# One core, two transformer layers in fp32: the first batch's query tiles go between its key steps, and the second batch's input is normalised late

## The chip, the cores and the metric

The program runs on one core of a Trainium2 chip. A core has TensorE (PE, matrix products, with the queue PEld for its weight loads), VectorE (DVE), ScalarE (ACT), GpSimd (POOL) and SyncE (SP, which here only issues DMAs). Each engine works through its own list of instructions in order, and semaphores tie the lists together. PE writes to PSUM, eight banks of 512 fp32 columns; POOL reads and writes SBUF only. The metric is the device time of one execution in microseconds. The kernel before took 934.42 us, the median of 3 runs (934.37 to 938.33).

## The reference

Two layers work on x, 2 batches of 1024 rows of 128. What the change touches is the attention of the first layer, on the input's layer norm:

```python
xn = _layernorm(x, ln_scale, ln_bias)
q = (xn @ Wq).reshape(b, n, HEADS, d).transpose(0, 2, 1, 3)      # 16 heads of 64
k, v = jnp.split(xn @ Wkv, 2, axis=-1)                            # 4 groups of 64 each
q = _layernorm(q, qn_scale, qn_bias)                              # per head
k = _layernorm(k, kn_scale, kn_bias)
dots = jnp.einsum('bghqd,bgkd->bghqk', qg, k) * d ** -0.5         # 4 heads share a group's keys
attn = jax.nn.softmax(dots, axis=-1)
out = jnp.einsum('bghqk,bgkd->bghqd', attn, v)                    # then out @ Wout, added to x
```

Behind it come a mixture of 8 experts (2 chosen per batch), a gated attention unit in chunks of 64 rows and a gated feed-forward layer with integer weights. They are the same in both kernels.

## The kernel before

Each batch goes through three stages, and the second batch's follow the first's.

**Head.** The rows are normalised over 128 columns (`normalise`, after a power -0.5 on POOL in `root`) and turned by PE (`turn_x`). Keys and values are made in four steps of 256 rows (s = 0 to 3): PE projects (`keys_values`, into two PSUM banks, `kv_at`), ACT squares the keys and keeps the values, DVE sums the squares of each head (`sum_keys`), ACT guesses the inverse root by a logarithm and an exponential (`guess_keys`), DVE mends the guess in three small instructions (`newton`) and multiplies (`normal_keys`, which writes every head twice, side by side: 1008 columns), PE turns the result (`turn_keys`), ACT keeps it rounded (`high_keys`, kh) and DVE the rest (`low_keys`, kl). Queries are made in eight tiles of 128 rows (j = 0 to 7): PE projects the centred weights (`norms`, whose squares give the rate) and the weights folded with the scales (`folded`); ACT squares, DVE sums, ACT guesses, and the product with the rate is made by DVE straight from PSUM for j = 0 to 3 (`normal_queries`) and by POOL for j = 4 to 7, from a copy that ACT makes (`keep_folded`, `rate`). Then PE turns (`turn_queries`), ACT keeps qh, DVE ql. In the first batch DVE also makes the biases (`shifts`), POOL folds the weights (`fold`), PE turns the later layers' weights (`turn_w`), and the second batch's input is normalised by POOL, turned and kept.

**Row maxima.** For j = 4 to 7 PE makes between the projections two score blocks each (`unit_scores`: 128 queries of two heads by 512 keys); DVE takes each block's largest (`largest`), two blocks give a row's maximum, and SP places it by DMA in ql, so that the exponent is taken of scores less their maximum.

**Attention.** 16 slots (`SLOTS`), each two query tiles of one group, in four phases, 64 and the overhang in all. A phase has on PE two score blocks, two key tiles of scores for an earlier slot (`tile_scores`, three products of high and low parts) and two of value products (`tile_values`); ACT takes the exponentials (`exps`), POOL adds them up in five adds of 1024 columns and one of a tail that DVE adds (`add_tail`). Four phases later PE adds up over the rows (`add_up`), ACT inverts (`invert`), DVE corrects and scales (`correct`, `scale`), PE projects (`project_out`), DVE adds to x (`add`). The order on each engine is written out by hand in its `produce` and `attention`; a phase number is `ph`, and slot m's key tiles start at ph = 4m + 5 (`LAG`).

## Time and profile before

| | |
|---|---|
| Median of 3 runs | 934.42 us |
| Profiled execution: time, span | 934.55 us, 932.8 us |
| Mean granted clock | 0.963 of full |
| PE busy | 849.1 us, 91% |
| DVE busy | 638.1 us, 68% |
| POOL busy | 548.5 us, 59% |
| ACT busy | 457.7 us, 49% |

The shares are means over stages that differ. The first batch's head and maxima lie from 5 to 98 us, its attention to 384, the second batch's head and maxima to 461, its attention to 755, and the later layers behind. The time outside the span is 1.75 us. A clock of 0.5 in a stretch is TensorE's lower level, 1.2 GHz, and 1.0 the upper, 2.4 GHz.

### The profile page before, as it was taken

Reading aid. Unit: us, or ns where it says so; the run is one execution under the profiler, and the core shown is the slowest. Engines: PE = TensorE matmul, PEld = TensorE weight load, DVE = VectorE, ACT = ScalarE, POOL = GpSimd, SP = SyncE. Lnnn points to the kernel's source line nnn. Section 1 sums busy time; section 2 is a strip of 40 time slices with the busy share of each in tenths; the row PEclk is TensorE's granted clock in tenths of the full one; section 3 lists DMA queues with packets and bytes.
Section 4 is the critical chain, followed back from the end, with each engine's and each line's share of the span. In section 5 each row is a group of like instructions: output and inputs, shape, how many; then the busy total and the mean of one; then the engine's idle time right before and its main releaser. Section 6 shows DMA issues by size and latency. Waiting matters only on the chain. (4 is left out here: it accounts for less than half of the span.)

```text
span 932.8 us, 13290 instructions
## 1 busy us (share of the span) xinstructions
PE 849.1 (91%) x4792; PEld 442.0 (47%) x4792; DVE 638.1 (68%) x1060; ACT 457.7 (49%) x822; POOL 548.5 (59%) x319
## 2 busy tenths in 40 slices
PE   2797999999999999989799999999999937998598
PEld 2554444444444444544444444444444413784355
DVE  6887667777777775488677777777776354255853
ACT  2465455555555556555455555555555514435232
POOL 3323688688868878403476887788778821247400
PEclk9899999999999999999899999999999966999799
DMA  5000000000000000000000000000000002000001
GB/s 161 1 0 1 1 1 1 1 2 1 1 1 1 1 1 2 1 1 1 1 1 1 2 1 1 2 1 1 1 1 1 1 26 68 1 2 0 0 1 46
DMA packets 49595, 7.96 MB, mean 9 GB/s; under 512 B 42486, under 2 KB 47994, under 8 KB 49530
## 3 DMA queue, kind: packets, MB, share of 16 engines
q1 hardware_dynamic: 48666, 6.99, 4.7%
q8 instruction: 38, 0.62, 0.3%
q14 instruction: 27, 0.22, 0.1%
q10 hardware_dynamic: 864, 0.13, 0.1%
HBM read 5.92 MB, written 1.05 MB: 7 GB/s over the span
## 5 line engine op out<-in xcount | busy, mean ns | idle before, releaser
L977 DVE TENSOR_REDUCE part<-psum 128x2 f32<-128x1024 f32 x256 | 313.3, 1224 | 137.5 <-PE psum L511 137.5
L399 POOL TENSOR_TENSOR space<-space 128x1024 f32<-128x1024 f32 x160 | 380.6, 2379 | 38.3 <-ACT space L752 20.5
L752 ACT ACTIVATE space<-psum 128x512 f32<-128x512 f32 x512 | 264.5, 602 | 156.4 <-PE psum L531 155.5
L546 PE MATMUL psum<-space,vb 128*64 128x512 f32 x1024 | 247.7, 605 | 0.0
L511 PE MATMUL psum<-kh,qh 64*128 64x512 f32 x512 | 128.5, 498 | 13.8 <-DVE part L977 13.4
L404 POOL TENSOR_TENSOR space<-space 128x1024 f32<-128x1024 f32 x30 | 71.6, 2385 | 106.2 <-DVE space L991 106.2
L511 PEld LDWEIGHTS psum<-kh,qh 64*128 64x128 f32 x512 | 48.2, 185 | 154.4 <-DVE part L977 120.3
L546 PEld LDWEIGHTS psum<-space,vb 128*64 128x64 f32 x1024 | 62.4, 136 | 106.5 <-issue 101.1
L531 PE MATMUL psum<-qh,kh 64*128 64x512 f32 x512 | 103.5, 401 | 0.0
L531 PE MATMUL psum<-ql,kh 64*128 64x512 f32 x512 | 102.4, 396 | 0.0
L531 PE MATMUL psum<-qh,kl 64*128 64x512 f32 x512 | 101.9, 394 | 0.0
L420 PE MATMUL psum<-wproj,xnt 128*128 128x512 f32 (+1 forms) x192 | 78.0, 544 | 0.9 <-DVE space L959 0.7
L1297 POOL TENSOR_TENSOR inv<-inv,half_power 128x4 f32<-128x4 f32 (+1 forms) x16 | 19.2, 1203 | 88.0 <-DVE inv L1581 76.4
L531 PEld LDWEIGHTS psum<-qh,kh 64*128 64x128 f32 x512 | 49.2, 189 | 12.9 <-issue 3.6
L531 PEld LDWEIGHTS psum<-qh,kl 64*128 64x128 f32 x512 | 49.1, 188 | 11.7
L531 PEld LDWEIGHTS psum<-ql,kh 64*128 64x128 f32 x512 | 48.9, 188 | 11.1
L420 PEld LDWEIGHTS psum<-wproj,xnt 128*128 128x128 f32 x192 | 35.9, 200 | 24.4 <-issue 20.4
L759 ACT ACTIVATE space<-psum 128x512 f32<-128x512 f32 x32 | 19.2, 601 | 56.2 <-PE psum L574 54.3
L991 DVE TENSOR_TENSOR space<-space 128x512 f32<-128x512 f32 x60 | 44.6, 746 | 2.9 <-ACT space L752 2.9
L766 ACT ACTIVATE space<-psum 128x512 f32<-128x512 f32 x32 | 19.2, 599 | 55.4 <-PE psum L561 55.4
L574 PEld LDWEIGHTS psum<-wout,space 128*64 128x64 f32 x512 | 30.0, 137 | 22.7 <-issue 17.1
L574 PE MATMUL psum<-wout,space 128*64 128x128 f32 x512 | 33.6, 273 | 4.5 <-DVE space L1006 4.5
(164 smaller groups left out, 887.6 us busy)
## 6 DMA issues: line engine op xcount, KB each, us to landing
ql<-nmx SPq DMA_DIRECT2D x256, 0.5 KB, 2.0
w1s<-in_L_ffn_W SPq DMA_DIRECT2D x4, 256.0 KB, 2.7
w2s<-in_L_ffn_W SPq DMA_DIRECT2D x4, 256.0 KB
out<-x SPq DMA_DIRECT2D x4, 256.0 KB, 2.1
x<-in_L_attn_x SPq DMA_DIRECT2D x2, 256.0 KB, 4.4
wproj<-in_L_attn_Wq SPq DMA_DIRECT2D x1, 512.0 KB, 6.7
x<-in_L_attn_x SPq DMA_DIRECT2D x1, 512.0 KB, 7.6
wout<-in_L_attn_Wout SPq DMA_DIRECT2D x1, 512.0 KB, 6.7
```

The source lines that it names most:

```text
L399: pool.tensor_tensor(to, pt[0] if u == 1 else to, pt[u], ALU.add)\
L404: pool.tensor_tensor(to, to, tail, ALU.add).then_inc(pool_added, 1)
L420: return pe.matmul(to, xnt[:, b, j * P:(j + 1) * P], wproj[:, first:first + to.shape[1]], start=True, stop=True)
L511: last = pe.matmul(scores[:, h * 512:(h + 1) * 512], qh[rows(h), PAIRS * g + hp, at * QB + t * P:at * QB + (t + 1) * P], kh[rows(h), g, ha ...
L531: last = pe.matmul(key_scores[kt % 2][h].rearrange("p (a q) -> p a q", a=PAIRS), key[rows(h), g, keys], queries(query[rows(h)], m), start= ...
L546: last = pe.matmul(outp[rows(h), :], vb[:, place(m)[1], kt, :], pt[kt][:, h, :], start=(kt == 0), stop=(kt == TILES - 1))
L574: last = pe.matmul(sums[rows(s), t * P:(t + 1) * P], ot[:, at:at + DH], wout[:, PAIRS * g + hp, :], start=(hp == 0), stop=(hp == PAIRS - 1))
L752: act.activation(pt[kt][:, h, :], key_scores[kt % 2][h], ACT.Exp).then_inc(exp_made, 1)
L759: act.activation(ot, outp, ACT.Copy).then_inc(out_kept, 1)
L766: act.activation(rinv, sums, ACT.Ln).then_inc(log_made, 1)
L977: dve.tensor_reduce(to[:, half, :], scores.rearrange("p (h k) -> p h k", h=2), AX_X, ALU.max, negate=True)\
L991: dve.tensor_tensor(tail[:, h, :], pt[TILES - 2][:, h, :], pt[TILES - 1][:, h, :], ALU.add).then_inc(tail_made, 1)
```

## The change

1. **Order of the first head.** `norms` and `folded` of tiles 0 to 2 go between the key steps; steps 2 and 3 of the first batch use PSUM banks 6 and 7, so that step 2 needn't wait. `shifts` moves in between the sums and the product of the fourth key step, the weights' turns behind the first and second query turns.
2. **GpSimd** normalises all eight query tiles (`normal`), and copies the keys' twins (`twin`); DVE's `normal_keys` writes 504 columns, and its `normal_queries` is gone. ACT makes `keep_folded` for all tiles.
3. **The second batch's input** is normalised by DVE in phases 64 to 66 of the first batch's attention, after a guess by ACT and DVE's three steps, turned by PE at the end of phase 67 and kept by ACT in phase 68.
4. **The first key tiles.** The first two key tiles of a batch and their exponentials go ahead of the last query turn; DVE takes the first maxima of slot 1 around `low_queries` of tiles 6 and 7.
5. **Order of the second head.** `norms(1, 0)` and `folded(1, 0)` stand ahead of the last keys' turn, and the wait for the last addition to x goes from `produce` to the first query turn.

On PE the second batch's input is turned in the head of the first batch (`L410` with `xnt`), between projections (`L420`), turns of weights (`L415`) and of queries (`L493`). In the kernel before:

```order
L420 MATMUL psum<-wproj,xnt 128x512 x2
L493 MATMUL psum<-ident,space 128x128 x8
L420 MATMUL psum<-wproj,xnt 128x512 x2
L410 MATMUL psum<-ident,xnt 128x128 x8
L420 MATMUL psum<-wproj,xnt 128x512 x2
L493 MATMUL psum<-ident,space 128x128 x8
L420 MATMUL psum<-wproj,xnt 128x512 x4
```

In the changed kernel the first head's list on PE reads (`L439` projects, `L471` turns keys, `L517` queries, `L434` weights):

```order
L471 MATMUL psum<-ident,space 128x128 x8
L439 MATMUL psum<-wproj,xnt 128x512 x2
L471 MATMUL psum<-ident,space 128x128 x8
L439 MATMUL psum<-wproj,xnt 128x512 x2
L439 MATMUL psum<-wproj,xnt 128x256 x4
L439 MATMUL psum<-wproj,xnt 128x512 x2
L471 MATMUL psum<-ident,space 128x128 x8
L439 MATMUL psum<-wproj,xnt 128x512 x4
L471 MATMUL psum<-ident,space 128x128 x8
L439 MATMUL psum<-wproj,xnt 128x512 x2
L517 MATMUL psum<-ident,space 128x128 x8
L434 MATMUL psum<-ident,space 128x128 x8
```

The projections between the key turns are those of tiles 0 to 2, and the turn of `xnt` is gone from there. It stands near the end of the first batch's attention, among key tiles (`L555`), value products (`L570`) and the output projection (`L598`):

```order
L570 MATMUL psum<-space,vb 64x512 x4
L429 MATMUL psum<-ident,xnt 128x128 x8
L555 MATMUL psum<-qh,kh 128x512 x2
L555 MATMUL psum<-ql,kh 128x512 x2
L555 MATMUL psum<-qh,kl 128x512 x2
L555 MATMUL psum<-qh,kh 128x512 x2
L555 MATMUL psum<-ql,kh 128x512 x2
L555 MATMUL psum<-qh,kl 128x512 x2
L570 MATMUL psum<-space,vb 64x512 x8
L598 MATMUL psum<-wout,space 64x128 x8
L439 MATMUL psum<-wproj,xnt 128x256 x8
```

Phases 68 and 69 are behind it on PE. On DVE the same place, from the correction of slot 13 (two instructions in PSUM and the scaling of `space`) to that of slot 14, reads before:

```order
L997 TENSOR_TENSOR psum<-psum,space 128x512
L1000 SCALAR_TENSOR_TENSOR psum<-psum,space 128x512
L1006 TENSOR_TENSOR space<-space,psum 128x512
L991 TENSOR_TENSOR space<-space 128x512 x2
L1015 TENSOR_TENSOR x<-x,psum 128x256
L997 TENSOR_TENSOR psum<-psum,space 128x512
L1000 SCALAR_TENSOR_TENSOR psum<-psum,space 128x512
L1006 TENSOR_TENSOR space<-space,psum 128x512
L907 MEMSET space 128x16 x2
```

and in the changed kernel, from the scaling of slot 13 on:

```order
L1071 TENSOR_TENSOR space<-space,psum 128x512
L932 BN_STATS stats<-x 128x6 x8
L935 BN_AGGR mv<-stats 128x2 x8
L939 TENSOR_SCALAR st<-mv 128x8
L1056 TENSOR_TENSOR space<-space 128x512 x2
L1080 TENSOR_TENSOR x<-x,psum 128x256
L989 SCALAR_TENSOR_TENSOR st<-st 128x8
L990 SCALAR_TENSOR_TENSOR st<-st 128x8
L991 SCALAR_TENSOR_TENSOR st<-st 128x8
L943 TENSOR_SCALAR xnt<-x,mv,st 128x128 x8
L1062 TENSOR_TENSOR psum<-psum,space 128x512
L1065 SCALAR_TENSOR_TENSOR psum<-psum,space 128x512
```

The moments stand ahead of the tail adds, the three rate steps and the eight scalings ahead of slot 14's correction. On POOL the head of the first batch reads now (`L357` is a twin, `L344`, `L347` and `L352` fold the weights, `L399` converts the integers):

```order
L338 TENSOR_TENSOR st<-st,root_power 128x8
L344 TENSOR_TENSOR space<-wproj,cross 128x1024
L357 TENSOR_SCALAR space<-space 128x8x64
L347 TENSOR_TENSOR wproj<-wproj,cross 128x1024
L357 TENSOR_SCALAR space<-space 128x8x64
L352 TENSOR_TENSOR wproj<-wproj,firsts 128x1024
L353 TENSOR_SCALAR wproj<-firsts 128x16
L357 TENSOR_SCALAR space<-space 128x8x64
L371 TENSOR_SCALAR q_rate<-q_rate 128x16
```

Twins stand between the three foldings, which stood in one piece before.

The core of the diff:

```diff
-        def kv_at(s):
-            return [banks(2 + 2 * (s % 2) + i, 1) for i in range(2)]
+        def kv_at(b, s):
+            first = (2, 4, 6, 6) if b == 0 else (2, 4, 2, 4)
+            return [banks(first[s] + i, 1) for i in range(2)]
...
+            def twin(b, s):
+                pool.wait_ge(kn_made, STEPS * b + s + 1)
+                pool.tensor_scalar(kn[s % 2][:, :, 1, :], kn[s % 2][:, :, 0, :], 1.0, 0.0, ALU.mult, ALU.add).then_inc(twin_made, 1)
...
+            def normal(b, j):
+                n = TILES * b + j
+                rate(j, n)
+                pool.wait_ge(u_kept, n + 1)
...
             def turn_keys(b, s):
-                pe.wait_ge(kn_made, n + 1)
+                pe.wait_ge(twin_made, n + 1)
                 if s:
                     pe.wait_ge(kh_made, n)
                     pe.wait_ge(kl_made, n)
...
             def attention(b, end):          # PE
+                    if b == 0 and ph == 4 * SLOTS + 3:
+                        pe.wait_ge(part_made, 8 * SLOTS)
                         pe.wait_ge(xn_made[1], 1)
                         turn_x(1, 0, TILES)
...
                 turn_queries(b, TILES - 2)
                 unit_scores(SLOTS * b + 1, 0)
                 unit_scores(SLOTS * b + 1, 1)
+                tile_scores(SLOTS * b, 0)
+                tile_scores(SLOTS * b, 1)
                 turn_queries(b, TILES - 1)
...
+                    if b == 0 and ph == 4 * SLOTS + 2:          # ACT, behind keep_out and invert
+                        act.wait_ge(var_made, 2)
+                        act.activation(st[:, 1, 3, :], st[:, 1, 0, :], ACT.Ln).then_inc(x_log, 1)
+                        act.wait_ge(x_log, 1)
+                        act.activation(st[:, 1, 2, :], st[:, 1, 3, :], ACT.Exp, scale=-0.5).then_inc(x_guess, 1)
...
-                low_queries(b, TILES - 2)
                 largest(SLOTS * b + 1, 0)
+                low_queries(b, TILES - 2)
                 largest(SLOTS * b + 1, 1)
+                largest(SLOTS * b + 1, 2)
                 low_queries(b, TILES - 1)
+                largest(SLOTS * b + 1, 3)
...
+                    if b == 0 and ph == 4 * SLOTS:              # DVE
+                        moments(1, 0, TILES)
+                        variances(1)
+                    if b == 0 and ph == 4 * SLOTS + 2:
+                        dve.wait_ge(x_guess, 1)
+                        newton(st[:, 1], 0.0, 1.0)
+                        normalise(1, 0, TILES)
...
             sum_keys(0, 2)                                      # DVE, first batch
+            first_sums()
+            first_columns()
             normal_keys(0, 2)
+            low_keys(0, 0)
+            sum_queries(0, 0)
             low_keys(0, 1)
             sum_keys(0, 3)
+            shifts()
             normal_keys(0, 3)
```

## Rows read from the trace of the kernel before

**Rows 1.** Windows of the span; columns: length, busy us (x instructions) per engine, clock, DMA.

```profile
14.38:59.99 45.61, 35.23 (x140) 23.08 (x140) 37.54 (x74) 22.65 (x38) 15.82 (x14) 0.93 0.06 8
...
81.81:98.11 16.30, 10.34 (x54) 6.85 (x53) 10.74 (x12) 6.36 (x12) 5.58 (x7) 0.80 0.03 2
98.11:377.58 279.47, 279.28 (x1742) 132.87 (x1740) 202.43 (x262) 153.22 (x291) 217.26 (x92) 1.00 0.04 1
377.58:383.62 6.04, 6.04 (x46) 3.06 (x44) 0.18 (x3) 2.06 (x4) 5.36 (x3) 1.00 0.00 0
383.62:422.21 38.59, 33.08 (x147) 19.07 (x145) 29.91 (x51) 19.95 (x37) 0.00 (x0) 1.00 0.00 1
...
444.03:460.74 16.71, 10.38 (x53) 7.26 (x53) 10.73 (x12) 6.15 (x12) 5.27 (x7) 0.80 0.03 0
```

**Rows 2.** Timeline of PE, head of the first batch; columns: start, us, instruction, idle before.

```profile
24.23 1.97 PE L449 MATMUL psum<-ident,space 128*128 128x128 f32 x8 [5.07 <-DVE space L932]
...
34.65 1.06 PE L449 MATMUL psum<-ident,space 128*128 128x128 f32 x8 [2.06 <-DVE kl L940]
35.55 1.88 PE L420 MATMUL psum<-wproj,xnt 128*128 128x512 f32 x4
...
59.99 0.50 PE L511 MATMUL psum<-kh,qh 64*128 64x512 f32 x2
```

**Rows 3.** Timeline of DVE, head of the first batch.

```profile
16.11 2.34 DVE L890 TENSOR_SCALAR shift<-cross 128x63 f32<-128x63 f32 x1
...
22.97 1.21 DVE L932 TENSOR_TENSOR space<-psum,k_rate 128x1008 f32<-128x1008 f32 x1
```

**Rows 4.** Timeline of POOL, head of the first batch.

```profile
16.04 2.35 POOL L343 TENSOR_TENSOR space<-wproj,cross 128x1024 f32<-128x1024 f32 x1 [5.10 <-DVE wproj L876]
...
29.81 1.91 POOL L346 TENSOR_TENSOR wproj<-wproj,firsts 128x1024 f32<-128x1024 f32 x1 [9.10 <-DVE firsts L902]
...
31.98 1.18 POOL L377 TENSOR_SCALAR space<-space 128x1152 f32<-128x1152 int32 x1
```

**Rows 5.** Timeline of PE, first batch, from production into attention.

```profile
87.31 0.50 PE L511 MATMUL psum<-kh,qh 64*128 64x512 f32 x2 [3.18 <-DVE part L977]
```

**Rows 6.** Groups by line, 0 to 98 us; columns: busy us, mean ns, idle before.

```profile
L710 ACT ACTIVATE space<-psum 128x1024 f32<-128x1024 f32 x8 | 8.2, 1026 | 7.7 <-PE psum L420 7.7
L386 POOL TENSOR_TENSOR space<-space,q_rate 128x1024 f32<-128x1024 f32 x4 | 7.6, 1904 | 0.3
...
L940 DVE TENSOR_TENSOR kl<-psum,kh 128x1024 fp32r<-128x1024 f32 x4 | 4.9, 1216 | 0.1
```

**Rows 7.** Timelines of PE, DVE, ACT and POOL, end of the first batch.

```profile
377.58 0.51 PE L531 MATMUL psum<-qh,kh 64*128 64x512 f32 x2
...
365.20 3.10 DVE L991 TENSOR_TENSOR space<-space 128x512 f32<-128x512 f32 x2 [1.47 <-ACT space L752]
...
369.98 0.60 ACT L759 ACTIVATE space<-psum 128x512 f32<-128x512 f32 x1 [1.36 <-PE psum L574]
...
370.78 9.95 POOL L399 TENSOR_TENSOR space<-space 128x1024 f32<-128x1024 f32 x4
380.89 2.36 POOL L399 TENSOR_TENSOR space<-space 128x1024 f32<-128x1024 f32 x1 [0.17 <-ACT space L752]
```

**Rows 8.** Timelines of DVE and POOL, the layer norms of the next layer.

```profile
757.75 2.36 DVE L1589 TENSOR_SCALAR y<-x,mv,inv 128x128 f32<-128x128 f32 x8
...
767.69 6.18 DVE L1589 TENSOR_SCALAR y<-x,mv,inv 128x128 f32<-128x128 f32 x8
...
757.92 1.03 POOL L1297 TENSOR_TENSOR inv<-inv,half_power 128x4 f32<-128x4 f32 x1 [0.28 <-DVE inv L1581]
...
768.87 4.92 POOL L1327 TENSOR_TENSOR xb<-x,beta 128x512 f32<-128x512 f32 x4
```

**Rows 9.** Windows with a lowered clock.

```profile
24.20:29.70 5.50, 5.47 (x18) 4.64 (x19) 4.69 (x9) 2.18 (x5) 0.00 (x0) 0.50 0.01 1
...
95.00:98.20 3.20, 3.20 (x18) 2.04 (x18) 1.23 (x1) 1.51 (x3) 1.31 (x2) 0.52 0.06 3
```

More of the change, by code:

```diff
@@ L426, in keys_values @@
                     pe.wait_ge(exp_made, 2 * TILES * SLOTS * b)
[L427 to L430 removed]
+                if n == 2:
+                    pe.wait_ge(xnt_made, 2)
+                if s == 3 or (b and s == 2):
+                    before = n if b == 0 else n - 1
+                    pe.wait_ge(kn_made, before)
+                    pe.wait_ge(v_made, before)
+                for first, to in zip((K_AT, V_AT), kv_at(b, s)):
                     for j in range(2):
@@ L644, in _ @@
             keys_values(0, 1)
+            keys_values(0, 2)
             turn_keys(0, 0)
-            keys_values(0, 2)
+            norms(0, 0)
             turn_keys(0, 1)
+            folded(0, 0)
             keys_values(0, 3)
+            norms(0, 1)
             turn_keys(0, 2)
+            folded(0, 1)
+            norms(0, 2)
+            turn_keys(0, 3)
+            folded(0, 2)
+            turn_queries(0, 0)
+            pe.wait_ge(w_float, 1)
+            pe.wait_ge(kh_made, STEPS)
+            pe.wait_ge(kl_made, STEPS)
+            turn_w(0, 8)
+            norms(0, 3)
+            turn_queries(0, 1)
+            folded(0, 3)
+            pe.wait_ge(w_kept, 1)
+            turn_w(8, W_TILES)
             produce(0)
             attention(0, 4 * SLOTS + LAG + 1)
+            pe.wait_ge(xnt_made, 3)
             keys_values(1, 0)
@@ L660, in _ @@
             turn_keys(1, 2)
-            pe.wait_ge(x_added, SLOTS)
+            norms(1, 0)
+            folded(1, 0)
+            turn_keys(1, 3)
+            norms(1, 1)
+            folded(1, 1)
+            norms(1, 2)
+            turn_queries(1, 0)
+            folded(1, 2)
+            norms(1, 3)
+            turn_queries(1, 1)
+            folded(1, 3)
             produce(1)
@@ L1109, in _ @@
             low_keys(1, 2)
+            sum_queries(1, 0)
+            low_keys(1, 3)
+            sum_queries(1, 1)
+            sum_queries(1, 2)
+            low_queries(1, 0)
+            sum_queries(1, 3)
+            low_queries(1, 1)
             produce(1)
```

275 lines of the change are left out of this document (141 added, 134 removed).

## The prediction

> **What bounds the kernel now.** I read the windows first. From 98.11 to 377.58 us, the attention of the first batch, TensorE (PE) is busy for 279.28 of 279.47 us [rows 1]: nothing moved there can pay, only less PE work could, and the change takes none away. The second batch is alike. The waits that a new order can fill stand in the production stretches: PE waits 10.4 of 45.61 us from 14.38 to 59.99, 6.0 of 16.30 us from 81.81 to 98.11, 5.5 of 38.59 us from 383.62 to 422.21, and 6.3 of 16.71 us from 444.03 to 460.74 [rows 1]. Next the timeline of PE: in the first of these it waits 5.07 us for the first normalised keys, and the clock is down afterwards, so that eight transposes take 1.97 us instead of 1.06 [rows 2]; in the second it waits 3.18 us for VectorE (DVE) at 87.31 [rows 5]. Between the batches, 377.58 to 383.62, PE has no wait at all [rows 1]: what the change puts there costs in full if it has to wait.
>
> **The sum's base** is the profiled execution, 934.55 us (span 932.8), 0.13 above the median of the runs, 934.42.
>
> **Head of the first batch.** I go through the four queues in the new order, each instruction starting at the later of its engine's turn and what it waits for, with durations of its row: 1.22 us for a VectorE pass over 1024 columns, 1.03 on ScalarE (ACT), 1.90 for the query product on GpSimd (POOL) [rows 6], 1.06 for eight transposes and 1.88 for a projection on PE (0.88 and 1.72 where the next overlaps) [rows 2]. The shifts leave the way of the first keys (they held DVE to 21.1, and mostly stood still behind POOL [rows 3, 4]), and the key product halves: 1.21 us for 1008 columns [rows 3] becomes about 0.7 for 504. The twin copy is new: between 0.2 us (a 16-column form) and 1.2 (1152 columns, row at 31.98 [rows 4]); nearest by size, 0.6. First keys then stand at 19.9, their turn on PE at 20.9 against 24.23, and the first query projection ends at 23.6. But three of DVE's short instructions with SBUF operands now meet a long one of POOL's, and the row at 16.11 says what that costs: 2.34 us for 63 columns, until POOL's 2.35 us instruction had ended [rows 3, 4]. The rate of the second keys (21.1) stands behind `scale_rest` (20.6 to 22.95), that of the third (26.0) behind `take_first` (1.91 us), and `low_keys(0, 0)`, queued behind both, ends at 30.1. So `turn_keys(0, 1)` starts only at 30.15, after 6.5 us of waiting and with the clock down: with its turn and the folded projection at half speed for part of the way, 35.0. From there: keep and guess 1.5, third step's square and sum 1.2, the shifts behind POOL's query product and its integer conversion until 41.4, rate and product 1.3, `sum_queries` and `low_keys(0, 2)` 2.3: `turn_keys(0, 3)` starts at 45.0. Then PE is full: five turns at 0.88, four projections at 1.72 and a wait of 0.4, 11.7 us, and the first scores start at 56.7 instead of 59.99 [rows 2]. **Gain 3.3 us.** Bounds: nothing (every queue slip on this path counts), and 9 us if DVE did not stand behind POOL at the three places (3.7 and 2.4 us of it).
>
> **Rows of scores.** From j = 4 to 7 both orders have the same six steps with the same waits: no change.
>
> **From production into attention, in both batches.** DVE now takes the first maximum of the second slot ahead of `low_queries(6)`, and PE the two key tiles ahead of `turn_queries(7)`. The second block of scores starts at 85.45 instead of 87.31, the key tiles at 86.7 (their maxima have to be placed by DMA first) instead of behind the second slot's second block, and what is then late is the alternation of scores and maxima, 1.8 us a block. By the same walk the seventh phase starts 2.95 us sooner. Against it: this stretch has the clock at half for two spells, 0.52 from 95.0 to 98.2 [rows 9], behind much shorter waits than the 3.18. If it is down under the first value products instead, up to 2.95 goes back. I take 2.0, nearer to the whole. **Gain 2.0 us twice**, bounds 0 and 2.95 each.
>
> The Trainium skill, TensorE: Matmul & The Clock Gate, in its part on the clock gate, ties the lowered clock to a long idle gap; by that the shorter waits of the new order keep the clock up, each gain is 2.95, and the time would be 932.2. The row at 95.0 speaks against taking it whole.
>
> **Head of the second batch.** It starts on PE as before, since the first eight projection pairs, the sums and the output projection fill it. The key turn 1 comes 1.0 us later (`low_keys(1, 0)` now behind three corrections), the rest sooner: the folded projection no longer waits for the last keys' turn, and rate and query product are off DVE (0.6 and 1.2 us a tile). Walked through: turn 2 at +14.8, folded projection at +17.7, first query turn at +26.1 (POOL's product ends at +26.05, so it is just hidden; if POOL were 1 us slower, so would this be), first scores at +34.8 instead of +38.59 [rows 1]. **Gain 3.8 us**, bounds 2.5 and 4.5.
>
> **End of the first batch: the late normalisation.** It was POOL's, early in the program; now it is on DVE, after ACT's guess, and PE must turn the result at the end of phase 67, when its own work is done at 377.5 [rows 7]. ACT can only give the guess after `keep_out(14)` (369.98 to 370.58 [rows 7]) and two short activations: 371.05. By then POOL is in the adds of the last slot, four back to back from 370.78 to 380.73 and one from 380.89 to 383.25 [rows 7]. DVE has three rate steps that read SBUF twice, then eight SBUF-to-SBUF scalings. What they cost beside such adds: eight scalings took 2.36 us with POOL nearly free, 6.18 with POOL in four adds of 1.23, the last four of them one per add [rows 8]; two tail adds of 512 columns, some 1.4 us of work, took 3.10 from 365.20, under a slot's last add [rows 7]. So one per add: the rate steps at 373.25, 375.7 and 378.2, the first scaling at 380.7, the second at 383.3, the other six behind it in 1.6 us: 385.0. PE waits from 377.5 to 385.0, 7.5 us, and comes back at half clock; after the 5.07 us wait it was at half for 5.5 us [rows 9], and the spells of 3.1 us are the other end, so half of that, 1.6 to 2.8, is lost: 2.3. The turn itself is 1.0. **Cost 10.8 us.** Nothing hides it, for the key tiles, two pairs of value products and the output projection of phases 68 and 69 stand behind the turn on PE, and the second batch behind them. Bounds: zero stall (cost 1.0, the turn) and 12.8.
>
> The Trainium skill, SBUF — State Buffer, § Who interferes with whom, gives a DVE instruction of these forms and a GpSimd one an exclusive hold for the whole instruction. The trace agrees for the adds, and not for the small power beside the first eight scalings: 1.03 us long, it cost them 0.2 [rows 8].
>
> **Sum**: 934.55 - 3.3 - 2 x 2.0 - 3.8 + 10.8 = 934.25; less 0.13, about 934.1. The turn's 1.0 us of PE was in the first head before and is counted there as gone.
>
> **Rivals.** (1) DVE slips between POOL's adds: the small power above cost it nothing much, and there are gaps of some 0.2 us between adds (9.95 us for four, 2.36 for one [rows 7]). Then the input is ready by 374, PE never waits, and of 10.8 only the turn's 1.0 us stays, which stands against it in the head: 934.1 - 9.8 = 924.3. Against it: 3.10, 2.34 and 6.18 us. (2) Slower: the clock. If it falls in each new wait, the transitions give nothing and the stall costs 12.8 us: 934.1 + 4.0 + 2.0 = 940.1. It decides when value products behind the score blocks take 3.7 us a pair instead of 1.8. (3) The new head of the first batch gives nothing, because the key chain (turn, high, low, turn) stays the last, now with foreign work in its queues: 934.1 + 3.3 = 937.4. For it: by the walk turn 1 comes only at 30.15, though turn 0 is 3.3 us sooner.
>
> **How the numbers follow.** Forecast 0.60, its own range 930 to 938.5; rival 1 0.18; rival 2 0.12; rival 3 0.10. A measurement of this kernel tells 0.5% (4.7 us) from no change. Faster by more than that (under 929.8): rival 1, and 0.06 for a head that gains near its upper bound: 0.24. Slower (over 939.1): rival 2 and 0.03 of the other two: 0.15. Same: 0.61. The range, 925 to 940.5, leaves out the better part of rival 1 and the edge of rival 2.
>
> **What would show it.** A PE wait of some 7.5 us before eight transposes near 372 to 380 (all is some 5 us sooner there), eight scalings on DVE taking over 6 us beside POOL's adds, and half clock behind it; first scores near 56.7; 34.8 us from the second batch's first projection to its first scores; rate steps stretched to about 2 us at 21 and 26. The prediction is wrong if the scalings take 2.4 us, or if PE's first wait for `kl` is gone.

## The result, and the profile after

The changed kernel takes 944.41 us, median of 4 runs (942.4 to 946.1), beside 934.39 for the kernel before: a ratio of 1.0091, 95% interval 1.0064 to 1.0118. It is slower by 8.5 us by the ratio, by 10.0 by the medians. The forecast was 934.1, next to no change, with a range of 925 to 940.5: the measured time lies above that range. The profiled execution of the changed kernel took 942.8 us, span 941.0, granted clock 0.953 (before 0.963).

Windows of the changed kernel, cut at the starts of its stages (columns as in [rows 1]): head of the first batch, its rows of scores and transition, its attention, its end, then the same for the second batch.

```profile
14.85:57.97 43.12, 33.91 (x132) 21.68 (x133) 28.70 (x41) 24.48 (x42) 20.32 (x32) 0.92 0.05 5
57.97:97.13 39.16, 32.11 (x128) 17.13 (x128) 27.96 (x29) 19.88 (x29) 16.36 (x28) 0.87 0.03 1
97.13:375.30 278.17, 277.61 (x1736) 132.69 (x1736) 207.04 (x280) 152.27 (x291) 216.00 (x92) 1.00 0.04 1
375.30:392.10 16.80, 10.10 (x61) 5.40 (x57) 10.18 (x13) 4.55 (x8) 6.98 (x3) 0.80 0.00 0
392.10:428.70 36.60, 34.27 (x147) 20.24 (x145) 22.06 (x35) 23.59 (x41) 11.63 (x23) 0.95 0.00 1
428.70:467.11 38.41, 31.35 (x129) 16.52 (x128) 27.96 (x29) 20.12 (x29) 17.51 (x31) 0.89 0.03 1
467.11:762.22 295.11, 290.85 (x1814) 138.43 (x1812) 205.03 (x266) 157.10 (x298) 222.58 (x94) 0.99 0.03 1
```

Against [rows 1]: the first head fell from 45.61 to 43.12 us; from the first scores to the first value products it took 38.12 us (59.99 to 98.11) and now 39.16; the second head fell from 38.59 to 36.60; its scores and transition went from 38.53 (422.21 to 460.74) to 38.41. The big loss is in the fourth row, where TensorE (PE) is busy for only 10.10 of 16.80 us. And the column of the clock is lower in every row but one.

The timeline of PE, changed kernel (columns as in [rows 2]); `L471` turns keys, `L535` is a score block, `L517` turns queries, `L429` turns the second input, `L598` projects out:

```profile
31.00 1.94 PE L471 MATMUL psum<-ident,space 128*128 128x128 f32 x8 [6.52 <-DVE kl L1016]
...
45.77 1.06 PE L471 MATMUL psum<-ident,space 128*128 128x128 f32 x8 [2.17 <-DVE kl L1016]
...
57.97 0.50 PE L535 MATMUL psum<-kh,qh 64*128 64x512 f32 x2
...
83.42 0.80 PE L535 MATMUL psum<-kh,qh 64*128 64x512 f32 x2 [1.39 <-DVE part L1042]
...
87.50 1.97 PE L517 MATMUL psum<-ident,space 128*128 128x128 f32 x8
...
93.79 0.79 PE L535 MATMUL psum<-kh,qh 64*128 64x512 f32 x2 [1.82 <-DVE part L1042]
...
383.60 1.94 PE L429 MATMUL psum<-ident,xnt 128*128 128x128 f32 x8 [6.70 <-DVE xnt L943]
...
403.32 1.47 PE L471 MATMUL psum<-ident,space 128*128 128x128 f32 x8 [2.02 <-DVE kl L1016]
404.72 1.97 PE L598 MATMUL psum<-wout,space 128*64 128x128 f32 x16
```

The walk of the first head held nearly to the row: key turn 1 was forecast at 30.15 and stands at 31.00 (the program's first PE instruction is 0.48 us later than in the profile of before), turn 3 at 45.77 for 45.0, the first scores at 57.97 for 56.7, with 59.99 before [rows 2]. The wait of 3.18 us [rows 5] is gone and 1.39 stands there, but the block behind it already runs at the lower clock (0.80 us for 0.50), and so do the query turn and the block at 93.79. The turn at 45.77, behind a wait of 2.17 us, runs at full clock (1.06 us). Five windows of the same kernel with a lowered clock; before, the place of the first had half as much of it, and that of the fourth none [rows 1]:

```profile
82.90:89.30 6.40, 5.45 (x22) 3.69 (x22) 2.95 (x4) 2.17 (x4) 1.27 (x2) 0.51 0.04 0
93.50:96.90 3.40, 3.11 (x16) 2.38 (x16) 1.62 (x3) 1.00 (x2) 0.00 (x0) 0.54 0.05 0
379.90:386.75 6.85, 3.15 (x14) 2.66 (x16) 5.58 (x11) 0.00 (x0) 2.53 (x2) 0.50 0.00 0
403.90:407.40 3.50, 3.50 (x23) 2.75 (x22) 2.70 (x6) 1.43 (x3) 0.62 (x1) 0.52 0.02 5
462.00:468.90 6.90, 5.50 (x22) 3.11 (x24) 4.12 (x6) 2.17 (x4) 2.22 (x1) 0.52 0.03 3
```

Summed over windows of 1 us from 14 to 480, PE is at the lower level for 20.4 us before and 37.7 after, and what it does there costs 9.6 and 14.2 us more than at the full clock (busy time times one minus the clock).

DVE and then GpSimd (POOL), changed kernel, at the two places where DVE was to stand behind POOL:

```profile
22.02 1.86 DVE L989 SCALAR_TENSOR_TENSOR k_rate<-k_rate 128x8 f32<-128x8 f32 x1 [0.61 <-ACT k_rate L733]
...
26.90 1.90 DVE L990 SCALAR_TENSOR_TENSOR k_rate<-k_rate 128x8 f32<-128x8 f32 x1
...
370.18 2.33 DVE L989 SCALAR_TENSOR_TENSOR st<-st 128x8 f32<-128x8 f32 x1 [0.61 <-ACT st L831]
372.55 0.17 DVE L990 SCALAR_TENSOR_TENSOR st<-st 128x8 f32<-128x8 f32 x1
372.75 2.29 DVE L991 SCALAR_TENSOR_TENSOR st<-st 128x8 f32<-128x8 f32 x1
375.08 8.37 DVE L943 TENSOR_SCALAR xnt<-x,mv,st 128x128 f32<-128x128 f32 x8
```
```profile
370.12 9.94 POOL L418 TENSOR_TENSOR space<-space 128x1024 f32<-128x1024 f32 x4
380.23 2.37 POOL L418 TENSOR_TENSOR space<-space 128x1024 f32<-128x1024 f32 x1 [0.17 <-POOL space L418]
```

Rate steps of eight columns take 0.17 us alone and up to 2.33 beside a long POOL instruction, and eight scalings 8.37. Both places are as forecast, with one difference: two steps (0.17 and 2.29) got through at one gap of POOL's, where I had counted one each, so the scalings end at 383.4, not 385.0.

### The profile page after: what moved, and what is told of

It reads as the page before. It is cut to its first block and busy times, and to the rows that moved or that the text cites. A ratio compares the mean times of both kernels' runs of the same rounds, so it can differ in the third digit from the quotient of the medians.

```text
span 941.0 us, 13355 instructions
## 1 busy us (share of the span) xinstructions
PE 855.1 (91%) x4792; PEld 445.4 (47%) x4792; DVE 634.1 (67%) x1039; ACT 464.7 (49%) x832; POOL 569.3 (61%) x366
## 5 line engine op out<-in xcount | busy, mean ns | idle before, releaser
L570 PE MATMUL psum<-space,vb 128*64 128x512 f32 x1024 | 248.3, 606 | 0.0
L535 PE MATMUL psum<-kh,qh 64*128 64x512 f32 x512 | 128.8, 499 | 12.6 <-DVE part L1042 12.1
L535 PEld LDWEIGHTS psum<-kh,qh 64*128 64x128 f32 x512 | 48.3, 185 | 153.0 <-DVE part L1042 117.8
L570 PEld LDWEIGHTS psum<-space,vb 128*64 128x64 f32 x1024 | 62.5, 136 | 107.1 <-issue 100.9
L555 PE MATMUL psum<-qh,kh 64*128 64x512 f32 x512 | 104.4, 404 | 0.8 <-DMA ql<-nmx 0.8
L555 PE MATMUL psum<-ql,kh 64*128 64x512 f32 x512 | 103.2, 399 | 0.0
L555 PE MATMUL psum<-qh,kl 64*128 64x512 f32 x512 | 102.6, 397 | 0.0
L439 PE MATMUL psum<-wproj,xnt 128*128 128x512 f32 (+1 forms) x192 | 78.0, 546 | 0.4 <-ACT space L755 0.3
L555 PEld LDWEIGHTS psum<-qh,kh 64*128 64x128 f32 x512 | 49.5, 190 | 14.1 <-issue 3.9
L555 PEld LDWEIGHTS psum<-qh,kl 64*128 64x128 f32 x512 | 49.5, 189 | 11.6
L555 PEld LDWEIGHTS psum<-ql,kh 64*128 64x128 f32 x512 | 49.3, 189 | 11.0
L439 PEld LDWEIGHTS psum<-wproj,xnt 128*128 128x128 f32 x192 | 36.0, 201 | 24.7 <-issue 20.7
L598 PEld LDWEIGHTS psum<-wout,space 128*64 128x64 f32 x512 | 31.4, 142 | 21.9 <-issue 17.5
L598 PE MATMUL psum<-wout,space 128*64 128x128 f32 x512 | 35.2, 282 | 3.5 <-DVE space L1071 3.5
```

Source lines behind the costliest of these rows:

```text
L439: return pe.matmul(to, xnt[:, b, j * P:(j + 1) * P], wproj[:, first:first + to.shape[1]], start=True, stop=True)
L535: last = pe.matmul(scores[:, h * 512:(h + 1) * 512], qh[rows(h), PAIRS * g + hp, at * QB + t * P:at * QB + (t + 1) * P], kh[rows(h), g, ha ...
L555: last = pe.matmul(key_scores[kt % 2][h].rearrange("p (a q) -> p a q", a=PAIRS), key[rows(h), g, keys], queries(query[rows(h)], m), start= ...
L570: last = pe.matmul(outp[rows(h), :], vb[:, place(m)[1], kt, :], pt[kt][:, h, :], start=(kt == 0), stop=(kt == TILES - 1))
L598: last = pe.matmul(sums[rows(s), t * P:(t + 1) * P], ot[:, at:at + DH], wout[:, PAIRS * g + hp, :], start=(hp == 0), stop=(hp == PAIRS - 1))
```

## The experiments

So the stall was where I had put it, and what failed was the clock or the order in the heads and transitions, the stretches from production into attention. Each table gives the ratio to the kernel before, 95% interval, from the same chip; 0.1% is 0.93 us.

### The parts apart

e1 takes root and scalings of the second input back to POOL, ahead of its first adds; e2 takes the old order at the end of production; e3 and e4 add one part each to the kernel before; e5 has neither, only the new heads.

```
e1, e5 (POOL, behind normal(0, 7)):
+    root(1); wait root_made
+    xn[1] = (x[1] - mean) * root          # 8 scalings
     (DVE: moments(1), variances(1) ahead of produce(0); late parts out)
e2, e5:  PE    -tile_scores(S*b, 0), -tile_scores(S*b, 1)   # before turn_queries(b, 7)
         ACT   -exps(S*b, 0), -exps(S*b, 1)
         DVE   low_queries(6); largest 0, 1; low_queries(7)  # largest 2, 3 behind
e3:  before + moments/variances/scalings in phases 64, 66, turn in 67, keep in 68
e4:  before + the sooner order (e2's lines, the other way)
```

| run | median us | ratio | interval |
|---|---|---|---|
| after | 944.41 | 1.0091 | 1.0064 to 1.0118 |
| e1 early normalisation | 932.87 | 0.9983 | 0.9967 to 0.9998 |
| e2 old transition | 940.84 | 1.0067 | 1.0045 to 1.0089 |
| e3 late normalisation alone | 944.15 | 1.0104 | 1.0080 to 1.0129 |
| e4 sooner order alone | 934.15 | 0.9995 | 0.9977 to 1.0012 |
| e5 new heads alone | 935.42 | 0.9984 | 0.9963 to 1.0006 |

> The changed kernel, with the second input normalised early: GpSimd takes root and eight scalings behind the last query product of the first batch, ahead of its first adds, from moments that VectorE makes before produce(0). TensorE's turn of that input stays at the end of phase 67. Theory 1 (the loss is the late normalisation standing behind GpSimd's adds): TensorE's wait of 6.70 us before the turn at 383.6 and the half clock behind it go, the turn's 1.0 to 1.1 us stays; the second batch's first projection starts 7.6 us sooner than in the changed kernel (384.5 against 392.1), the median is 944.4 - 7.6 = 936.8. Rival (GpSimd's added pass or VectorE's moments ahead of the first adds push the start of attention by some 2 us, so that the first batch's attention gives back what the stall cost): 939 or more, with the seventh attention phase later than 99.0. Second rival (the wait only moves, because at the end of the first batch TensorE is ahead of GpSimd's adds anyway): over 941.

> The changed kernel, with the order of the kernel before at the end of each production stretch (key tiles, exponentials and the third and fourth maximum of the second slot back behind the last query turn, on TensorE, ScalarE and VectorE). Theory 1 (the new order at this place is itself what lost: the clock falls under the key tiles and again under the first value products): the time falls by what the two traces lost there, 0.9 and 0.6 us, to 942.9, and the lowered clock near 84 to 89 us is gone. Theory 2 (the order gains 2 us a batch, as forecast, but the new heads hand over a lowered clock which took it away): the time rises by some 2 to 4 us, to 946.5 to 948.4. If neither, within 0.5 us of 944.4.

> The kernel before, with the late normalisation of the second input alone (moments at phase 64 and scalings at phase 66 on VectorE, guess on ScalarE, turn at the end of phase 67 on TensorE). Theory 1 (it stands on its own as the greatest loss): first projection of the second batch 9.2 us later relative to phase 67, less the 1.0 us that the turn no longer takes in the head: 934.4 + 8.2 = 942.6. Rival (the stall in the changed kernel was made worse by its new head, because GpSimd runs later against TensorE there): 934.4 + 4, 938.4, with a wait of under 4 us before the turn.

> The kernel before, with the sooner key tiles and maxima of the change at the end of each production stretch, and nothing else. My prediction had this at a gain of 2.0 us in each batch: 930.4. Theory 1 (the order itself loses, by the clock): 934.4 + 0.9 + 0.6 = 935.9, with a stretch at half clock under the value products near 98. Theory 2 (only the new heads' clock spoiled it): 930.4 to 932, with the seventh attention phase near 98.1 instead of 100.16.

> The changed kernel with both undone: the second input normalised early on GpSimd, and the old order at the end of each production stretch. What is left of the change are the two new heads (query tiles between key steps, GpSimd's query products and twin copies). If the parts add (early normalisation gave -11.5 us on the changed kernel, the old transition -3.6), it comes to 944.4 - 11.5 - 3.6 = 929.3. If the old transition only gave its 3.6 us because there the lowered clock fell elsewhere by chance, then it is that of the early normalisation alone, 932.9. My prediction's terms for the heads (3.3 and 3.8, less the turn's 1.0 us, which stays at the end of the batch) say 934.4 - 6.1 = 928.3.

The late normalisation costs 9.7 us on the kernel before (e3) and 10.1 on the changed one (1.0091 less 0.9983): theory 1, and more than the 8.2 and 7.6 expected. In e3's profile 10.4 us are added between the first value products and the second batch's first projection (295.95 us for 285.51 before), 1.0 of it the turn, and 1.5 us behind that. The sooner order gives nothing: 0.5 us less on the kernel before, 0.1 less on the new heads (e1 against e5), and 2.2 more in the changed kernel (against e2, intervals overlap); my 4.0 is out of reach of e4's interval. The new heads give 1.5 us, where the terms said 6.1 (3.3 and 3.8, less the turn); e5's interval includes no gain at all, and its upper end is 3.5. The parts add up: 9.7 - 0.5 - 1.5 = 7.7, measured 8.5.

Twelve runs of e5, one program, lie from 927.63 to 936.57, and their granted clocks from 0.967 to 0.956: three at 0.961 or more, all under 930.3, and nine at 0.959 or less, all over 935.1. The forecast for the heads (928.3) is what they take in the executions with the highest clock (927.63 and 928.21 at 0.967). Summed over windows as above, what PE does at the lower level costs 12.8 us more than at the full clock in e5's profile (935.87 us), 3.2 more than before.

### The stall taken away, and its clock alone

```
e6 (POOL):  for the last slot of batch 0, columns 0:1 instead of 0:512 of each half in the running sum
            (the rest of that sum is left out)
e7 (PE), ahead of wait(xn_made[1]) at the end of phase 67:
+    for _ in range(6):
+        for h in range(8): transpose(banks(0, 2)[h], ident, ident)   # thrown away
```

| run | median us | ratio | interval |
|---|---|---|---|
| e6 no long adds in the last slot | 928.15 | 0.9933 | 0.9909 to 0.9957 |
| e7 stall filled | 938.53 | 1.0028 | 1.0009 to 1.0048 |

> The changed kernel, where GpSimd's seven-fold running sum of the first batch's last slot adds one column instead of 512 in each half (the sum is left out, its semaphores stay). The late normalisation stays on VectorE. Theory 1 (VectorE's rate steps and scalings stand behind GpSimd's long adds, one per add): the three steps and eight scalings from 370.2 to 383.5 take under 3.5 us, TensorE's wait of 6.70 us before the turn goes wholly, and the time falls by the stall and its half clock, 8.4 us, to 936, or, as with the early normalisation, by 11.5 to 933. Rival (the guess comes too late, or VectorE's own queue is the limit): the wait stays over 3 us, and the time over 940.

> The changed kernel, with 48 idle transposes of the identity on TensorE (6 times 8, some 5.6 us at full clock) ahead of the wait for the late normalisation, so that TensorE works through most of its 6.70 us wait; their results are thrown away. Theory 1 (part of the loss is the clock that the wait brings down: the turn at 1.94 instead of 1.06 us and some 3 us of projections at half speed behind it): 944.4 - 2.4 = 942. Theory 2 (the wait also unsettles the clock later, in the second batch's head and transition, where runs with the stall all show spells): 940. Rival (the clock has nothing to do with it, only the wait counts): within 0.5 us of 944.4.

DVE and PE in e6: all three rate steps at 0.17 us, eight scalings in 2.14 instead of 8.37, and no wait ahead of the turn.

```profile
365.89 0.17 DVE L990 SCALAR_TENSOR_TENSOR st<-st 128x8 f32<-128x8 f32 x1 [0.61 <-ACT st L832]
...
366.49 2.14 DVE L944 TENSOR_SCALAR xnt<-x,mv,st 128x128 f32<-128x128 f32 x8
```
```profile
372.51 1.09 PE L430 MATMUL psum<-ident,xnt 128*128 128x128 f32 x8
```

That settles the mechanism: the guess comes in time, DVE's queue is free, and POOL's adds are what holds DVE. The gain of e6, 14.8 us, is larger than either number I gave, and 4.7 us larger than that of e1. Of this, 0.8 is e1's own price: the first batch's stage from first scores to value products is longer by that where POOL makes the extra pass (37.48 us in e10 below, against 36.66 in e9, which lacks the pass, all at full clock). The other 3.9 us are not shown to be the stall's. In the two profiles, 3.2 us apart, e6's first head is 3.5 us shorter than e1's (43.78 for 47.28 from PE's first turn) and the stage behind it 2.2, both long before the slot that e6 edits; e1 has a low spell at 45 to 49 that e6 lacks.

PE in e7: the wait is down to 1.26 us and the turn back at 1.09.

```profile
379.19 5.46 PE L628 MATMUL psum<-ident 128*128 128x128 f32 x48
385.91 1.09 PE L429 MATMUL psum<-ident,xnt 128*128 128x128 f32 x8 [1.26 <-DVE xnt L946]
```

Transposes that do nothing make the kernel 5.9 us faster (1.0091 to 1.0028; the ends of the two intervals leave 1.5 to 10.2), with the input ready as late as before. That is nearer to theory 2 than to theory 1. From the turn to the second batch's first projection it takes 7.07 us instead of 8.50, so 1.4 is won there; the rest must be won in stages whose low spells move from run to run (in its profile the second batch's scores and transition took 36.65 us for 38.41).

### The keys first in the new head

```
e8 = e5 and   DVE:  first_columns, low_keys(0, 0), normal_keys(0, 2), sum_queries(0, 0), shifts, low_keys(0, 1), ...
              POOL: normal(0, 0), twin(0, 3), integer conversion
```

> As the run with the new heads alone, and in the first head low_keys(0, 0) ahead of the third keys' rate steps, the shifts into VectorE's idle time ahead of low_keys(0, 1), and GpSimd's last key twin ahead of the integer conversion. Theory (the second key turn waits 6.6 us because its VectorE predecessor is queued behind a rate step that is itself stuck 1.90 us behind GpSimd, and the fourth because of 3.6 us of shifts): turn 1 of the keys starts 2.7 us sooner relative to the first, turn 3 some 2 us more, first scores 3 to 5 us sooner, and the time is that of the new heads alone less 3 to 4.5 us: 925 to 929. Rival (the key product, which reads SBUF too, gets stuck in its turn beside GpSimd's 1.90 us subtraction, so only the order of the stuck ones changes): within 1 us of the new heads alone.

Median 927.11 us, ratio 0.9922 (0.9902 to 0.9941): 5.8 us under e5, faster than both kernels. Timelines of DVE, POOL and PE:

```profile
26.26 1.23 DVE L1013 TENSOR_TENSOR kl<-psum,kh 128x1024 fp32r<-128x1024 f32 x1 [0.31 <-ACT kh L743]
```
```profile
26.04 1.91 POOL L352 TENSOR_TENSOR wproj<-wproj,firsts 128x1024 f32<-128x1024 f32 x1 [1.18 <-DVE firsts L976]
```
```profile
27.63 1.94 PE L477 MATMUL psum<-ident,space 128*128 128x128 f32 x8 [3.98 <-DVE kl L1013]
```

The low keys read PSUM and SBUF, and took 1.23 us inside POOL's 1.91 us instruction, beside which the changed kernel's rate step, two SBUF operands, took 1.90. The wait for them fell from 6.52 to 3.98 us; the first head took 38.34 us against 43.12. The rival (they would be stuck in their turn) falls.

### The clock held

These keep PE busy in its waits with idle transposes (`fill`, eight of them about 0.9 us) into banks that are free.

```
e9  = before + fill x5 ahead of turn_keys(0, 0); x3 between unit_scores(S*b+1, 0) and (.., 1)
e10 = e5     + fill x6 ahead of turn_keys(0, 1); x3 as e9
e11 = e8     + fill x4 ahead of turn_keys(0, 1); x3 as e9
e12 = e8     + the change's sooner order, no fill
e13 = e11    + fill x1 ahead of unit_scores(S*b+1, 3), x1 behind it
e14 = e12    + fill x4 ahead of turn_keys(0, 1); x1 behind unit_scores(S*b+1, 0), (.., 2), (.., 3)
e15 = e14    + 12 idle transposes ahead of turn_keys(1, 1)
e16 = e15    + low_keys(1, 0) ahead of scale(SLOTS - 1) on DVE
```

| run | median us | ratio | interval |
|---|---|---|---|
| e9 before, filled | 933.77 | 0.9980 | 0.9965 to 0.9995 |
| e10 new heads, filled | 927.56 | 0.9925 | 0.9900 to 0.9949 |
| e11 keys first, filled | 923.90 | 0.9864 | 0.9840 to 0.9888 |
| e12 keys first, sooner order | 928.42 | 0.9922 | 0.9900 to 0.9945 |
| e13 e11, short waits filled | 921.12 | 0.9851 | 0.9828 to 0.9874 |
| e14 sooner order, filled | 921.07 | 0.9851 | 0.9829 to 0.9874 |
| e15 second head filled | 917.92 | 0.9823 | 0.9797 to 0.9849 |
| e16 low keys ahead of scaling | 918.71 | 0.9822 | 0.9796 to 0.9847 |

> The kernel before, with idle transposes of the identity on TensorE in its three longest waits: 40 (4.4 us) ahead of turn_keys(0, 0), where it waits 5.07 us, and 24 (2.7 us) between the two first score blocks of the second slot in each production stretch, where it waits 3.18 us; their results are thrown away. Theory 1 (TensorE's clock falls behind such waits, and a low stretch of 3.4 us costs some 1.6 us of busy TensorE): the low stretches near 24 to 30 and 88 to 92 and 450 to 454 go or shrink; 3.0 us of the first, 1.6 and 1.5 of the others: 934.4 - 6 = 928.4 at best, 931 if the clock then falls later instead. Rival (low stretches come whatever TensorE does in its waits): within 1 us of 934.4, with as much low time in the first 480 us as before (20 us).

> The new heads alone (late normalisation and sooner transition undone, 935.4), with idle transposes in the waits: 48 (5.3 us) ahead of turn_keys(0, 1), where TensorE waits 6.6 us, and 24 in each production stretch as in the run on the kernel before. This is the test of where the heads' gain went. Theory 1 (the clock took it): with the clock held in both, the new heads are 5 to 6 us faster than the kernel before with its waits filled, as my walk said (3.3 + 3.8 - 1.0), and the spread between 927.6 and 936.6 of the unfilled heads closes at its lower end: 925 to 928. Rival (the heads gain less by their queues, the clock is level): no more than 2 us better than the filled kernel before.

> The new heads with low_keys(0, 0) and the shifts moved (927.1), with idle transposes in the waits: 32 (3.6 us) ahead of turn_keys(0, 1), where TensorE waits 3.98 us, and 24 in each production stretch. Theory 1: the low stretches at 27.5 to 31 and 80 to 85 go, 1.5 to 3 us each: 922 to 925. Rival (the clock falls later instead, under the first value products, or the idle work delays the real): 926 to 929.

> As the new heads with low_keys(0, 0) and the shifts moved (927.1), and the change's sooner key tiles and maxima at the end of each production stretch. If the sooner order gains nothing by itself (the two comparisons so far: 934.2 against 934.4 on the kernel before, 932.9 against 935.4 on the heads): within 1 us of 927.1. If it gains the 2.0 us a batch that I forecast and only the clock hid it: 923 to 925.

The windows of e10, its first head, scores and transition, second head, scores and transition; and the first two of e9:

```profile
14.22:54.99 40.77, 37.02 (x182) 25.42 (x182) 30.59 (x54) 24.48 (x42) 20.30 (x32) 1.00 0.07 10
54.99:92.47 37.48, 31.04 (x152) 17.07 (x152) 30.11 (x35) 19.63 (x29) 24.05 (x36) 1.00 0.03 1
378.77:413.79 35.02, 32.69 (x148) 19.05 (x146) 21.96 (x35) 23.59 (x41) 11.59 (x23) 1.00 0.00 1
413.79:450.44 36.65, 31.06 (x153) 17.07 (x153) 28.15 (x29) 19.69 (x29) 17.01 (x30) 1.00 0.03 1
```
```profile
14.12:59.82 45.70, 38.87 (x181) 26.50 (x181) 37.57 (x74) 22.30 (x38) 15.80 (x14) 0.96 0.07 11
59.82:96.48 36.66, 31.03 (x153) 17.07 (x153) 29.17 (x30) 19.70 (x29) 14.24 (x25) 1.00 0.03 1
```

With idle work in both, the heads are worth 0.55%, 5.1 us, for the 6.1 of my walk and the 1.5 of e5: theory 1. POOL's extra pass, which is in e5 and e10 and not in the changed kernel, takes 0.8 of it away. In rows: the second head at full clock takes 35.02 us, 3.6 less than before (38.59), forecast 3.8; the first 40.77 against e9's 45.70, 4.9 less, forecast 3.3 with a low spell in it. A low spell of 3.4 us stays in e9's first head, but next to nothing of it is in the 45.70, as its key turns show against the turns before, at 34.65 [rows 2] and here:

```profile
38.79 1.06 PE L449 MATMUL psum<-ident,space 128*128 128x128 f32 x8 [1.35 <-DVE kl L940]
```

and in e9:

```profile
34.21 1.94 PE L454 MATMUL psum<-ident,space 128*128 128x128 f32 x8 [3.19 <-DVE kl L948]
...
38.62 1.07 PE L454 MATMUL psum<-ident,space 128*128 128x128 f32 x8
```

The spell begins behind the wait of 3.19, and the wait of 1.35 that stood ahead of the next key turn takes it up. The old first head takes 45.61 us with 6.8 us of low clock (before) and 45.70 with 3.4 (e9): its key chain, not PE's speed, sets its length. The old second head is alike: 38.59 us at full clock, and 38.71 with a spell of 3.4 us in the profiles of e3 and e4. The new heads have fewer waits behind the spell, and there it counts in full. This is also why the kernel before gains only 1.9 us from its filling, less than the 3.4 to 6 I expected: its time is the one that my rival named (within 1 us of 934.4), though its low clock is half as much (10.3 us for 20.5). Another spell runs from 454 to 461, behind two waits of 1.47 and 1.32 us that I hadn't filled. e12 is level with e8 by the ratios: its first case, no gain from the sooner order.

> The filled kernel with the keys first (923.9), with 8 more idle transposes in each of the two waits of 1.3 to 1.5 us that stand behind the third and the fourth score block of the second slot, in both batches. Theory 1 (short waits bring the clock down too, as its profile had it low from 86 to 93): the low stretches there go in most runs, 1.6 us each: 921 to 923. Rival (waits under 1.5 us don't matter): 923.9 within 1 us.

> As e13, but with the change's sooner order at the end of each production stretch, whose waits are 1.39, 1.39 and 1.83 us: 8 idle transposes in each, and 32 ahead of turn_keys(0, 1). Theory 1 (the sooner order is worth 2.0 us a batch, and the clock took it): 4 us under e13, 917 to 919. Theory 2 (it is worth nothing by itself): within 1 us of e13. Theory 3 (in the new order the clock falls whatever fills its waits, because more of them are short and follow each other): 2 us or more over e13.

PE in e13, the second slot's first scores and the seventh phase's, and the same two in e14 (both at full clock in between):

```profile
75.38 0.49 PE L546 MATMUL psum<-kh,qh 64*128 64x512 f32 x2
...
90.29 0.50 PE L546 MATMUL psum<-kh,qh 64*128 64x512 f32 x2
```
```profile
75.47 0.49 PE L546 MATMUL psum<-kh,qh 64*128 64x512 f32 x2
...
89.24 0.50 PE L546 MATMUL psum<-kh,qh 64*128 64x512 f32 x2
```

Filling two waits of 1.5 and 1.3 us brought 921.12 from 923.90, ratios 0.9851 and 0.9864, so the difference may be chance; e13's profile has no low spell at all from 14 to 480, and neither has e10's. The sooner order is 13.77 us for 14.91 there, worth 1.1 us a batch, not 2.0 and not nothing. Yet e14 is no faster than e13 over all, since one more low spell stands in its second head, from 386 on.

> As e14 (921.1), with 12 idle transposes (1.5 us) on TensorE in the second batch's head, in its 2.02 us wait ahead of turn_keys(1, 1). Theory 1 (this wait brings the clock down in most runs, for 1.7 us of busy TensorE, which is why e14 is no faster than e13): the low stretch at 386 to 389 goes, the second head takes 35.0 us instead of 36.6, and the time falls by 1 to 2 us, to 919 to 920. Rival (the low stretch there is an accident of the one profile): 921.1 within 0.5 us.

> As e15, with low_keys(1, 0) ahead of the scaling of the output on VectorE, so that turn_keys(1, 1) comes 0.6 us sooner; the scaling is hidden by that turn. If the key chain sets the start of the second batch's scores: 0.6 us under e15. If TensorE is full behind it anyway, as in the old order's walk: the same as e15, since only the wait changes; the 12 transposes would then end just in time.

The second head and its key turn in e14, and then in e15:

```profile
373.86:410.45 36.59, 34.26 (x147) 20.17 (x145) 22.05 (x35) 23.59 (x41) 11.59 (x23) 0.95 0.00 1
...
385.08 1.28 PE L482 MATMUL psum<-ident,space 128*128 128x128 f32 x8 [2.02 <-DVE kl L1032]
```
```profile
373.70:408.73 35.03, 34.01 (x159) 20.42 (x158) 21.97 (x35) 23.61 (x41) 11.64 (x23) 1.00 0.00 1
...
384.93 1.06 PE L482 MATMUL psum<-ident,space 128*128 128x128 f32 x8 [0.71 <-DVE kl L1035]
```

The spell and 1.56 us are gone with the wait of 2.02. But the same unfilled wait left the clock up in other runs, as in e1:

```profile
395.02 1.06 PE L477 MATMUL psum<-ident,space 128*128 128x128 f32 x8 [2.02 <-DVE kl L1017]
```

Of the twelve profiles that have this wait unfilled, seven have the spell behind it and a head of 36.6 us (after, e2, e5, e7, e11, e12, e14), five have neither and take 35.0 (e1, e6, e8, e10, e13). So a single profile of e15 doesn't show that the filling removed it; its time, under that of e14, points the same way. e15, ratio 0.9823, is level with e16 as the fastest of all, 16.5 us under the kernel before; it does the whole computation. Against e14 it is 2.6 us by the ratios, with intervals that overlap. e16's order changes nothing: PE is full behind that turn.

## Why the prediction was wrong

| term | forecast | by itself, in runs | at full clock, in rows |
|---|---|---|---|
| heads, less the turn | -6.1 | -1.5 (e5) | -4.9, -3.6, less the turn |
| transitions, both | -4.0 | -0.5 (e4), 0 (e12 against e8) | -1.1 each |
| late normalisation, with the turn at the end | +9.8 | +9.7 (e3) | |
| sum | -0.3 | +7.7 | |

Taken apart, the forecast's sum is off by 8.0 us (7.7 for -0.3): 4.6 in the heads and 3.5 in the transitions, and 0.1 the other way in the late normalisation.

**The late normalisation** was right in mechanism and in sum, the sum in part by luck. Its stall was sized 7.5 us and was 6.70; the clock behind it was sized at 2.3, and between the turn and the first projection it cost 1.4 (8.50 against 7.07 us) in the changed kernel and 2.1 in e3; what makes up the rest of the 9.7 is spread over later stages. Rival 1 (DVE slips between the adds) is refuted by the rows at 370 and 375.

**From production into attention** is one step that failed: "I take 2.0, nearer to the whole", with the lower bound "If it is down under the first value products instead, up to 2.95 goes back". The sooner order replaces waits of 3.18, 0.68 and 1.32 us by waits of 1.39, 0.42, 1.39 and 1.82, and in the changed kernel the clock was low for 6.8 us from the first on and 3.4 behind the last, where before two spells of 3.4 stood. The walk itself was right, but it was set against the wrong row. From the second slot's first block to the seventh phase it took 16.53 us before (83.63 to 100.16), so the walk's 2.95 meant 13.58, and e14 has 13.77 at full clock. But the 16.53 hold the old order's own two low spells. With the clock held up the old order takes 14.88, as e9 shows:

```profile
83.47 0.50 PE L516 MATMUL psum<-kh,qh 64*128 64x512 f32 x2
...
98.35 0.50 PE L516 MATMUL psum<-kh,qh 64*128 64x512 f32 x2
```

So 1.65 of the 2.95 was the clock and not the order, which gives 1.1; and with its own low spells the new order took 17.47 (81.53 to 99.00). I had seen in [rows 9] that a spell began at 95.0 behind waits under 1.4 us, called it an argument "against taking it whole", and still took two thirds. The Trainium skill's TensorE: Matmul & The Clock Gate ties, in its part on the clock gate, the lower level to long idle gaps, though it also reports one kernel whose frequent short idles made the clock swing. The first is not borne out by these rows: the clock fell behind waits of 1.39 and 2.02 us. In e13, e15 and e16, where most such waits are filled, no profile has it low from 14 to 480.

**The heads** are the larger miss. Their timing walk holds (first head 4.9 us less in e10, whose clock is 1.00 there, where it said 3.3 with a low spell; second 3.6 for 3.8), and the step that failed is that I priced the clock only where a wait was new or long, and nowhere behind the heads. The second head gets its wait of 2.02 us from `low_keys(1, 0)`, which I had seen come "1.0 us later" and costed at nothing; in the changed kernel it is followed by a spell at 403.9 that costs 1.6. Before, that head had waits of 0.87, 0.91, 1.22 and 1.69 us and the clock at 1.00 throughout [rows 1], and where a spell did fall in it (e3, e4) it cost 0.1, since a later wait took it up. The first head trades a 5.07 us wait [rows 2] for one of 6.52 and another of 2.17. Behind the 2.17 the clock stayed up in the changed kernel and fell in the profiles of e1 and e7, whose heads are the longest (47.28 and 47.51 us from PE's first turn); behind the old head's 2.06, 1.35 and 1.90 it stayed up before. What the runs showed in place of the 6.1: 1.5 with the clock as it falls (e5), 5.1 with idle work holding it (e10 against e9). Rival 3 (the first head gives nothing) was wrong in its reason: the head did give 2.0 us in the profile.

**Rival 2**, the slower side, named the cause that came true, with 940.1 and a chance of 0.12. It let only the transitions and the stall lose, not the heads. Its test, value products at 3.7 us a pair behind the blocks, was too narrow: in the first batch it is the key tiles and the query turn that lose, and only in the second do the first value products stand in a low window.

What stays open: how much of the 3.9 us between e6 and e1 is chance, and what in each execution decides behind which of the short waits the clock falls, since runs of one program differ.

## What to carry to other kernels

Where PE waits in short pieces between bursts, a schedule that is 2 us shorter on paper can be level. Compare like with like: the rows of the old order hold its own low spells, and a walk at full clock set against them books the clock as gain (1.65 of 2.95 us here). Ask of each spell whether a wait behind it takes it up: an order with fewer waits pays for it in full. A new wait is then a chance of losing 1.5 to 1.7 us and not a sum (the wait of 2.02 us cost it in seven of twelve profiles), so look at the spread of one program's runs beside their granted clocks. Fill such waits with idle transposes into a free bank, in both orders, before judging an order; that shows what the order itself is worth. Before work with two SBUF operands is put on VectorE, see which long GpSimd instruction runs then, and let the instruction on the chain that reads PSUM go first.

## What was not expected of the hardware

- Low clock came in spells of about 3.4 us or twice that (93.50 to 96.90 and 403.90 to 407.40; 82.90 to 89.30 and 379.90 to 386.75), and a 3.4 us spell over busy PE with no wait behind it costs some 1.6 us: 36.59 against 35.03 for the second head. With waits behind it, it cost 0.1 (38.71 against 38.59, e3 and before).
- One program's times spread by 9 us (e5), with the granted clock between 0.956 and 0.967. The unchanged first head of the changed kernel took 43.8, 43.9, 45.3 and 47.5 us from its first turn to its first scores in four profiles (e6, e2, after, e7).
- Work for nothing made PE finish sooner: 5.5 us of idle transposes in a stall took 5.9 us off the kernel (e7).
- DVE's reduction of one SBUF operand ran at 1.22 us (46.02 in the changed kernel) and its subtraction of SBUF from PSUM at 1.23 (26.26 in e8) beside POOL's instructions of 1.90; rate steps with SBUF operands alone took up to 2.33 us for 0.17, and eight scalings 8.37 for 2.14.
